# Attention's beginning: the low halves of V and of the output weights on GpSimd, and V's first projection ahead of the first keys' transposes

## What is computed

```
x = x + attention(layernorm(x))        # 16 heads, rotary positions, 90 of 256 keys kept
x = x + long_conv(ctx, ctx, layernorm(x))
x = x + moe(layernorm(x))              # 12 experts, top 3
```

```
q, k, v = h @ Wq.T + bq, h @ Wk.T + bk, h @ Wv.T + bv
q, k = rope(q), rope(k)
p = softmax(q @ k.T / sqrt(32))        # keys 0..25 and the last 64
out = (p @ v) @ Wo.T + bo
```

## Time and profile before

| | |
|---|---|
| three runs | 1473.38, 1473.56, 1476.54 us (median 1473.56) |
| profiled execution, first to last instruction | 1471.8 us |
| TensorE busy | 1362.8 us, 93% |
| VectorE busy | 827.3 us, 56% |
| GpSimd busy | 845.1 us, 57% |
| ScalarE busy | 698.6 us, 47% |
| chain that ended last | PE 62%, DMA 2%, others 0% |

### The profile page before, as it was taken

How to read it: one execution, slowest core, us unless ns; L and a number is a source line. 1 busy time by engine, 2 the same in 40 slices (tenths; PEclk the granted TensorE clock), 3 DMA queues, 4 the chain that set the end, 5 groups by cost and what they waited for, 6 DMA issues and landing times.

```text
span 1471.8 us, 27775 instructions
## 1 busy us (share of the span) xinstructions
PE 1362.8 (93%) x7868; PEld 1136.4 (77%) x7869; DVE 827.3 (56%) x1197; ACT 698.6 (47%) x1878; POOL 845.1 (57%) x955
## 2 busy tenths in 40 slices
PE   5999998799998279999999999999999999999993
PEld 4777776577776268888888888888888888888883
DVE  7788887499998884746174444647443453000013
ACT  3657666154555225444454444445444454444530
POOL 0456545254564067767577676777767777565640
PEclk9999998899998579999999999999999999999985
DMA  7000000163334435545254444446444443251246
GB/s 272 1 1 0 0 0 27 49 213 100 105 112 150 152 107 131 139 123 143 60 156 112 107 100 121 120 116 163 103 117 93 128 114 79 37 155 36 33 132 235
DMA packets 77576, 152.42 MB, mean 104 GB/s; under 512 B 9120, under 2 KB 13728, under 8 KB 77024
## 3 DMA queue, kind: packets, MB, share of 16 engines
q1 hardware_dynamic: 62496, 115.09, 25.0%
q0 software_dynamic: 14320, 35.40, 12.3%
q10 hardware_dynamic: 720, 1.44, 0.3%
HBM read 119.31 MB, written 32.59 MB: 103 GB/s over the span
## 4 chain that ended last, share of the span: by engine, by line
PE 62%; DMA 2%; DVE 0%; SPq 0%; issue 0%; ACT 0%; DVEq 0%; POOL 0%; POOLq 0%
PE ps_h L1961 9%; PE ps_h L1962 9%; PE ps_h L1966 9%; PE ps_y L1984 9%; PE ps_y L1985 9%; PE ps_y L1988 9%; PE ps_td L1974 4%; PE ps_xd L1946 2%; DMA w_lo<-acc 1%; DMA xg<-xnd,gidx 0%; PE ps_xd L1995 0%; DMA acc<-y,si 0%; SPq L1670 0%; DVE w_lo L1751 0%; DVE w_lo L1782 0%
## 5 line engine op out<-in xcount | busy, mean ns | idle before, releaser
L1961 PE MATMUL ps_h<-w_hi,xh 128*128 x708 | 249.5, 363 | 1.4 <-ACT xh L1877 1.4
L1962 PE MATMUL ps_h<-w_lo,xh 128*128 x708 | 244.2, 356 | 0.0
L1984 PE MATMUL ps_y<-w_hi,hh 128*128 x590 | 237.1, 402 | 0.0
L1985 PE MATMUL ps_y<-w_lo,hh 128*128 x590 | 231.4, 392 | 0.0
L1686 DVE TENSOR_TENSOR w_lo<-stage,w_hi 128x512 f32 x220 | 214.5, 975 | 28.6 <-DVE w_hi L1684 2.9
L1819 POOL TENSOR_TENSOR y<-y,b_sb 128x512 f32<-128x512 f32 x58 | 81.9, 1411 | 209.0 <-ACT y L1902 209.0
L1809 POOL TENSOR_TENSOR hl<-h,hh 128x1280 fp32r<-128x1280 f32 x59 | 182.8, 3098 | 16.9 <-ACT hh L1896 16.5
L1883 ACT ACTIVATE h<-ps_h 128x512 f32<-128x512 f32 x177 | 80.6, 528 | 199.7 <-POOL hl L1809 190.8
L1902 ACT ACTIVATE y<-ps_y,wt 128x512 f32<-128x512 f32 x59 | 40.6, 689 | 274.8 <-PE ps_y L1988 274.8
L1966 PE MATMUL ps_h<-w_hi,xl 128*128 x708 | 164.9, 355 | 0.0
L1892 ACT ACTIVATE h<-ps_td,b_now 128x128 f32<-128x128 f32 x590 | 159.2, 394 | 3.9 <-PE ps_td L1974 1.2
(11 more groups left out here) (256 smaller groups left out, 2570.7 us busy)
## 6 DMA issues: line engine op xcount, KB each, us to landing
stage<-in_wcat SPq DMA_DIRECT2D x220, 256.0 KB
front<-in_ctx_rev SPq DMA_DIRECT2D x32, 192.0 KB, 2.4
w_lo<-in_wcat SPq DMA_DIRECT2D x4, 1280.0 KB, 12.1
acc<-added_c POOLq DMA_DIRECT2D x1, 4352.0 KB, 17.4
front<-kpad SPq DMA_DIRECT2D x16, 256.0 KB, 3.5
toe<-kpad SPq DMA_DIRECT2D x16, 256.0 KB, 3.6
x2d<-xs SPq DMA_DIRECT2D x16, 256.0 KB, 2.4
xnd<-xn_c SPq DMA_DIRECT2D x16, 256.0 KB, 2.0
```

The costliest lines, as they stand in the source:

```text
L1961: nc.tensor.matmul(out, x_hi, part(w_hi, e, k * FF + lo, hi - lo), start=(k == 0), stop=False)
L1962: nc.tensor.matmul(out, x_hi, part(w_lo, e, k * FF + lo, hi - lo), start=False, stop=False)
L1984: nc.tensor.matmul(ps_y[:], h_hi, part(w_hi, e, KD * FF + k * D, D), start=(k == 0), stop=False)
L1985: nc.tensor.matmul(ps_y[:], h_hi, part(w_lo, e, KD * FF + k * D, D), start=False, stop=False)
```

## The change

The low halves of Wv and Wo are no longer made by VectorE but by GpSimd (`split_vo`), with the same subtraction in the same two pieces, and counted on a new semaphore, `vo_split`. GpSimd does the two of V behind `first_std(0)` and the two of the output weights behind `first_std(1)`; each waits for ScalarE's rounded half. V's first projection stands between the queries' and the keys' transposes of batch 0 on TensorE; it was behind the scores. Both calls of `split_w` for these weights are gone from VectorE. ScalarE's and SyncE's orders stay.

```diff
+            def split_vo(j):
+
+                for f in range(2):
+                    part = slice(f * KD * D // 2, (f + 1) * KD * D // 2)
+                    pool.wait_ge(w_rounded, 2 * j + f + 1)
+                    nc.gpsimd.tensor_tensor(wlo[j][:, part], raw[j][:, part], whi[j][:, part].bitcast(F32),
+                                            ALU.subtract).then_inc(vo_split, 1)
...
             pool.wait_ge(c_in, 16)
+            split_vo(WV_)
             first_std(1)
+            split_vo(WO_)
             batch(0, False, True)
...
                 add_bias(b + 1, 2)
-                if first:
-                    split_w(WO_)
                 if x_next:
...
                 rope_first(j)
-            split_w(WV_)
             stats_of(1, 0)
...
                     if first and k % 2 == 0:
-                        pe.wait_ge(w_split, 2 * j + k // 2 + 1)
+                        if j < WV_:
+                            pe.wait_ge(w_split, 2 * j + k // 2 + 1)
+                        else:
+                            pe.wait_ge(vo_split, 2 * (j - WV_) + k // 2 + 1)
...
-            for j in range(3):
-                qk_t(0, j)
+            qk_t(0, 0)
+            qk_t(0, 1)
+            project(0, 3)
+            qk_t(0, 2)
             scores(0, 0)
-            project(0, 3)
```

More of the change, by code:

```diff
@@ L161, in attention @@
         xn_ready = sem("xn_ready")
-        w_rounded, w_split = sem("w_rounded_a"), sem("w_split")
+        w_rounded, w_split, vo_split = sem("w_rounded_a"), sem("w_split"), sem("vo_split")
         xh_ready, oh_ready = sem("xh_ready_a"), sem("oh_ready")
```

## The result

The changed kernel takes 1477.64 us (median of 7 runs, 1475.18 to 1480.36); the kernel before, run beside it, took 1472.68 (median of 7, 1472.19 to 1476.54). The ratio is 1.0026, with a 95% interval of 1.0015 to 1.0036: slower by 2.2 to 5.3 us. The profiled execution has a span of 1475.9 us where the one before had 1471.8, that is +4.1, against a forecast of +4.7. The ratio says +3.8 us and the two medians +5.0, so the three measures of one change lie 1.2 us apart, with the forecast between them.

What follows compares the result with a forecast made beforehand. TensorE, 93% busy, bounds the kernel, and the change is decided before 65 us. Terms +3.3 + 2.7 + 1.7 - 3.0 = +4.7 us took the median of 1473.56 to 1478.3, range 1470.5 to 1482.

Steps and rivals of the forecast that it cites:

- the mechanism is the one that it put first: Main case, chance 0.56: GpSimd's subtractions block VectorE's rotations and softmax scale, delaying TensorE before the loop; +4.7 us.
- A half on GpSimd takes 2.4 us and shuts VectorE out to its end: Each of four 128x1024 subtractions on GpSimd: 2.4 us, during which a contending VectorE instruction waits until it ends.
- The prediction's second figure, 2.2 us: Alternative length of one GpSimd half, from the skill's cycle estimate; it would make the sum +4.0.
- V's halves delay the rotations by 4.2 us: Batch 0's rotations on VectorE: two blocks of 2.1 us by GpSimd's V subtractions; bounds 0 and 4.8.
- V's projection from 28.4, 4.30 us: TensorE: runs until 32.7, keys' transposes wait; first maximum +4.7 us, less 1.4 idle, +3.3 at batch 1's x transposes.
- The 3.00 that the prediction set beside it: Length in us of V's projection at the upper clock level, set against 4.30.
- The output weights cost 1.3 and 1.4 us: GpSimd's two output-weight halves block VectorE's first and second softmax scales; together +2.7 us, bounds 0 and 4.8.
- The clock's ramp, 1.7 us: Batch 1's query projections start at the lower clock after a hole of over 6 us; bounds 0 and 2.5.
- 3.0 us come back: TensorE's 2.52 us hole before the probabilities' transposes and their slow run (1.5) go, less GpSimd's rotations; bounds 2.5, 3.5.
- B: Rival, chance 0.17: the port costs as forecast, but TensorE's clock stays up; +1.7 us, 1475.3.
- C: Rival, chance 0.17: GpSimd and the rotations read side by side, nothing blocks; -5.2 us, 1468.4.
- D: Rival, chance 0.10: VectorE keeps the port through its chain, GpSimd gets in only at 26.4; +2.3 us, 1475.9.

Runs made afterwards that it cites:

- y1: Kernel before, only the output weights' low halves moved to GpSimd, behind a wait for VectorE's second scale of the first tile; 1470.66 us, ratio 0.9983.
- x2: Changed kernel with all four GpSimd subtractions replaced by same-size writes of zeros that read nothing; 1468.03 us, ratio 0.9970.
- x1: Changed kernel with V's first projection back behind the first scores, the four subtractions staying on GpSimd; 1473.43 us, ratio 1.0006.
- x4: Changed kernel with idle filling matmuls put into TensorE's two long holes, results unused; 1475.53 us, ratio 1.0013.
- y4: Kernel before with only TensorE's order changed: V's projection ahead of the keys' transposes, all low halves still on VectorE; 1477.06 us, ratio 1.0026.
- z1: y2 with 6 and 7 idle filling matmuls on TensorE, behind the first scores and behind the next transposes; 1469.20 us, ratio 0.9968.
- y3: y1 without the wait: GpSimd subtracts the output weights right after the inverse root of batch 1; 1473.41 us, ratio 1.0000.
- y2: y1 plus V's projection ahead of the keys' transposes, V's low halves made by VectorE between second and third rotation; 1470.34 us, ratio 0.9982.
- y2_again: The same kernel as y2, run and profiled once more; 1470.22 us, ratio 0.9979.

## Why the prediction was right

It said 1478.3 us, slower by more than 0.2%, and the median is 1477.64; the mechanism is the one that it put first, with several of its steps off in place or size. The ratio, 1.0026, has an interval that reaches down to 0.15%. The forecast of +4.7 was added to a median of 1473.56; the one beside the changed kernel was 1472.68, so the time agrees to 0.7 us and the difference of the medians, 5.0, to 0.3.

- **A half on GpSimd takes 2.4 us and shuts VectorE out to its end.** Shown. 4.95 and 4.63 us for two (4.69 in y1, where nothing is in their way); a multiply of 0.42 lasts 2.65. The prediction's second figure, 2.2 us, was a little short. x2 settles for the rotation that it is the reading: with only writes its instructions keep their lengths. That is also the rule of the Trainium skill, "SBUF — State Buffer", section "Who interferes with whom", which says that an instruction of VectorE with two inputs in SBUF contends with one of GpSimd that reads SBUF, not with one that only writes it.
- **V's halves delay the rotations by 4.2 us.** They delay them by 4.4 (30.74 and 0.42, less 26.4 of the earlier trace rows, less the 0.4 of the later keys' weights). The places were wrong. I had the first half ahead of the first multiply; it is so in x1 and x4, but here V's weights came 0.8 us later. I had the second at VectorE's own wait after the third multiply, since "back-to-back VectorE instructions are not interrupted". They are: GpSimd's second half got in between the second and the third multiply. I had that sentence from one row, the 3.33 us of the earlier trace rows; y4 shows the same two subtractions letting GpSimd in, and why they did not in the earlier trace rows stays unsettled. As the count of blocks and the length of each are the same, the sum was not touched.
- **V's projection from 28.4, 4.30 us.** It starts at 29.07, with no wait for its low halves, and takes 5.15 (34.22 less 29.07), since all of it runs at the lower level; in the earlier trace rows the last five of the 12 matmuls ran near or at the upper one. Term mis-sized by 0.85, but x4, the same kernel up to there, has 4.14: the size of this term changes from execution to execution. (The 3.00 that the prediction set beside it runs to the end of the last matmul; from start to next start it is 2.85, 23.61 to 26.46 in x2.) With the later start this makes the first maximum late by 6.1 (36.47 against 30.36), where I had 4.7; 0.4 of it are the later keys' weights. The 1.4 us of VectorE's idle time went as foreseen: V's addition at 42.53 follows without a wait.
- **The output weights cost 1.3 and 1.4 us.** The scale loses 1.0 (1.18 less 0.17), and the second half does not come after the normalisations and meet the second scale, but falls into the pair of normalisations, which loses 2.1 (3.09 less 1.00, the pair's length in z1): 3.1 for 2.7. Again GpSimd got in sooner than I let it. The transposes of x, forecast for 42 to 43, start at 44.14.
- **The clock's ramp, 1.7 us.** 1.66, shown by x4. The size is right, the cause was put in the wrong place: the prediction counts it to the output weights' blocks, but x2 has a ramp of 1.71 without a subtraction, and x1 has none with both. It is the price of V's new place, which leaves TensorE empty behind the scores; blocks alone can bring it too, as y3 shows. The transposes of x at 44.14 take 1.08 us (0.63 before).
- **3.0 us come back.** 3.6 do: the shift falls from 9.3 to 5.65 at the mark. Of this 2.2 are the hole (2.52 less the 0.29 that stays) and 1.25 its slow transposes (3.41 less 2.16); my 3.0 had subtracted something for GpSimd's rotations, and TensorE waits for none of that.

So the shift at the mark is 7.6 and 1.7 less 3.6, +5.65, where the sum had +4.7: the chain to the first maximum and the blocks came out 1.4 and 0.4 larger, what comes back 0.6 larger, and the last 0.25 I can't place. 0.4 of the 5.65 are the keys' weights and not the change. What brought the profiled span back to +4.1 is a step that I did not have. Behind the loop TensorE's timeline ends attention like this before:

```profile
264.76 0.47 PE L741 MATMUL bank<-wo_hi,oT_hi 128*128 128x512 f32 x1 [0.81 <-ACT oT_hi L347]
...
268.02 1.32 PE L745 MATMUL bank<-wo_hi,oT_lo 128*128 128x512 f32 x4
```

and like this after:

```profile
269.86 0.47 PE L751 MATMUL bank<-wo_hi,oT_hi 128*128 128x512 f32 x1 [0.81 <-ACT oT_hi L347]
...
271.80 1.09 PE L755 MATMUL bank<-wo_hi,oT_lo 128*128 128x512 f32 x4
```

The last output projection takes 3.26 us to its final group before (268.02 less 264.76) and 1.94 after: one ran mostly at the lower level, the other at the upper. The shift, already down from 5.65 to 5.1 in the loop, goes to 3.8 there; at the end of the span it is 4.1. One kernel can have either: y2 has 3.02 us at this place and y2_again 1.93. Whether the change makes one of them more frequent is open. This is one reason why the runs of one kernel lie as far apart as they do (1467.9 to 1477.7 for the one before), and no forecast from one profiled execution can be surer than that. That errors of this size cancelled here (+1 at the mark, about -1.5 behind it) is luck.

**The rivals.** B fell with the rows at 29.07 and 44.14, both at the lower level; x4 gives the price of the second. C fell at the first multiply beside GpSimd. x2 comes near to what it would have been, -4.5 where I had worked out -5.2; C had no ramp in its sum. D fell with the rows at 19.14 and 21.71: VectorE does not keep GpSimd out through its chain.

## What to carry to other kernels

An idle engine is a free place for work only if it shares nothing with the engine on the path (here 4.7 us of VectorE work became 9.6 us on GpSimd, and 7.5 of them were taken from VectorE, at worse places): when work is put on GpSimd beside a chain of VectorE, name the VectorE instructions that will stand next to it, count one whole GpSimd instruction for each one that can get in (however short the VectorE instruction is), and hold it back by a semaphore until VectorE reads PSUM or idles: one such wait was worth 0.17% here. A matmul moved ahead to fill a hole fills it only if its last operand is there when the hole begins (y4) and if it is no longer than the hole (5.15 us in one of 1.8 here). And look at the place that it leaves: the hole there cost 1.3 to 2.7 us of clock.

## What the runs showed of the hardware that was not expected

- GpSimd does not wait for a gap in VectorE's sequence. Its next subtraction comes in between two VectorE instructions that follow each other at once, and the one behind it then lasts up to 2.2 us longer: 2.52 and 2.57 in x1, 2.65 and 2.82 after, 1.18 and 3.09 behind the maximum, 2.38 for an instruction of 0.17 in y3. In the earlier trace rows two VectorE subtractions held GpSimd off until both were over, in y4 the same two did not.
- A GpSimd write alone (0.92 us for 128x1024) leaves a subtraction with two SBUF inputs at 0.43 us, but VectorE's scale, which has one tensor input, lasts 0.80 beside it instead of 0.17 and ends at 30.44, when the second write does (28.58 and 1.84). The 1.43 of the pair behind it is no second block: its row starts before the scale is over. x2 shows the block, not its reason.
- The clock's level at one place is not fixed by the kernel alone. In y2_again V's projection stayed at the upper level after holes of 0.89 and 0.69 us; in z1, alike up to there but with later weights, it fell at the third matmul after holes of 1.44 and 0.69. In the changed kernel and in x4, also alike up to there, V's projection took 5.15 and 4.14.
